# Masks of the windowed attention: from TensorE matmuls to the VectorE instruction that finds the row maximum

## The chip, the cores and the metric

The kernel runs on one core of one Trainium2 chip. The metric is the device time of one execution in microseconds (us). The version before the change takes 2654.65 us, the median of three runs (2653.8 to 2655.82). Times inside an execution are read from one profiled execution.

## The reference, cut to what matters

The program is two transformer-like layers. The change touches only the second attention, a windowed one: 4,096 rows, 16 heads of 64, windows of 128 queries, and each window attends to itself and to the window before it.

```python
sim = jnp.einsum('bhwid,bhwjd->bhwij', bq, bk)       # 128 queries x 256 keys
causal_mask = (bq_t < bq_k) | (bq_t > bq_k + ws * LOOK_BACKWARD)
sim = jnp.where(causal_mask | pad_mask, mask_value, sim)
attn = jax.nn.softmax(sim, axis=-1)
out = jnp.einsum('bhwij,bhwjd->bhwid', attn, bv)
```

So of the window before, a query sees the keys from its own position on, of its own window the keys up to its own position, and the first window of a sequence has nothing before it.

## The kernel before

The last stage, `stage_windows`, goes over 32 tiles of 128 rows (one tile is one window, all 16 heads). Heads are taken in 8 pairs. The engines run programs of their own that meet through semaphores; `window_steps` writes one list of steps that all of them follow, and the order on every engine is that of this list.

- Step `S p` (the scores of head pair p): TensorE writes 128 x 2 heads x 256 keys into one of two PSUM tiles, `pss[p % 2]` (printed as w_pss). For each half of the keys (role 0 the window before, role 1 the own window) it first multiplies the mask by the identity (L1687), which puts 0 or -1e30 into the scores, and then adds three products of the high and low parts of q and k (`PARTS`, L1689). VectorE takes the negated row maximum of both heads (L1879), and ScalarE then computes exp(score + that) with the row sum (L1791), one instruction for each head.
- The scores buffer is double, so `S p` waits until the exponentials of pair p-2 are done: `wait(pe, exp_ready, PAIRS * t + max(p - 1, 0))`.
- `N p`: VectorE takes the reciprocal of the row sums (L1885), GpSimd scales the probabilities (L1626). `T p`: TensorE turns them (L1709), VectorE (even p) or ScalarE (odd p) copies them to SBUF. `PV p`: product with v (L1730).
- `W 0..5` and `E 0..3`: projections of the next tile (L1649 with wqkv) and of the experts of this tile (L1649 with we). They stand between the S steps. ScalarE empties W (L1748), VectorE empties E (L1900, L1902). `QR`, `KR`: rotation of the next q and k on VectorE and GpSimd (L1540, L1544, L1547). `R`: their transposes (L1661), taken by ScalarE (L1757, L1761) and VectorE (L1858, L1862).
- The end of a tile: `G` and `OUT`, the output product (L1739, w_psy) on TensorE, and on VectorE the gate (L1919 to L1921) and the result (L1926, L1930). VectorE's next instruction is the maximum of `S 0` of the next tile.

The tiles are visited by a generator, `tiles`. Tiles 0 and 1 are written out, tiles 2 to 29 are a loop with two tiles in its body (semaphore values in registers), tiles 30 and 31 are written out with shorter lists of steps. The last tile has no W steps.

Of the kernel before, what the change touches and what calls it, by code (L numbers as in the profile page):

```python
# [16 lines left out]
BF16 = mybir.dt.bfloat16  # L17
# [3 lines left out]
ALU = mybir.AluOpType  # L21
# [12 lines left out]
H = 16  # L34
EPS = 1e-5
NEG = -1e30


HD = D // H
# [1424 lines left out]
def stage_windows(nc, io, keep, dram, out):  # L1464
# [6 lines left out]
    with ExitStack() as ctx:  # L1471
        st = Stage(nc, ctx, "w_")
        wqkv, we, wout = keep["wqkv"], keep["we"], keep["wout"]
        rope = st.sb("rope", [P, 2, 3, DH // 2])
        own_mask = st.sb("own_mask", [P, P], BF16)
        before_mask = st.sb("before_mask", [P, P], BF16)
        even_masks = st.sb("even_masks", [P, NT // 2, P], BF16)
        xnt = st.sb("xnt", [P, 2, KD, P])
        xr = [st.sb(f"xr{r}", [P, 2, KD, P], F32R) for r in range(2)]
        x1 = st.sb("x1", [P, 2, D])  # L1480
# [40 lines left out]

        def tiles(eng):

            for i in rounds(eng, NT // 2 - 1):
                for u in range(2):
                    yield 2 * i + u, u, i, steps
            yield NT - 2, 0, NT // 2 - 1, ending_steps
            yield NT - 1, 1, NT // 2 - 1, last_steps

        def heads(ap):  # L1530
            return ap.rearrange("p (h s x) -> p h s x", s=2, x=DH // 2)
# [45 lines left out]
        @block.gpsimd  # L1577
        def _(pool):
            ch = Chain(pool, pool_step)
            def low_rows(tile, u):  # L1580

                pool.wait_ge(x_high, tile + 1)
                pool.tensor_tensor(xr[1][:, u, :, :], xnt[:, u, :, :], xr[0][:, u, :, :].bitcast(F32), ALU.subtract  # L1583
                                   ).then_inc(x_ready, 1)

            def rotate(n, t, taken, table, landed):

                if n == 0:

                    pool.wait_ge(rope_landed[table], landed)  # L1590
                    wait(pool, work_taken["act"], taken)
                    wait(pool, t_ready, turns.filled(t))
                    wait(pool, k_rotated, t + 1)
                ins = rotary(pool, 1, n, table)
                if n < 5:
                    ch.link(ins)
                else:
                    ins.then_inc(k_rotated, 1)

            low_rows(0, 0)  # L1600

            ch.link(pool.memset(own_mask[:, :], 0.0))
            ch.link(pool.affine_select(out=own_mask[:, :], in_=own_mask[:, :], compare_op=ALU.is_ge, fill=NEG, base=0,
                                       pattern=[[-1, P]], channel_multiplier=1))
            for mask in (before_mask[:, :].unsqueeze(1), even_masks[:, :, :]):
                ch.link(pool.memset(mask, 0.0))
                ch.link(pool.affine_select(out=mask, in_=mask, compare_op=ALU.is_ge, fill=NEG, base=0,  # L1607
                                           pattern=[[0, mask.shape[1]], [1, P]], channel_multiplier=-1))
            for b in range(B):

                ch.link(pool.memset(even_masks[:, b * NT // B // 2, :], NEG))

            pool.memset(v[1][:, :], 0.0).then_inc(pool_set, 1)

            low_rows(1, 1)
            pool.wait_ge(pool_set, 1)
            for n in range(6):
                rotate(n, -1, 4, 0, 16)
            start = ch.k
            for t, u, i, order in tiles(pool):  # L1620
                ch.base, ch.k = start + t * 5, 0
                for s in order:
                    if s[0] == "N":
                        p = s[1]
                        wait(pool, inv_ready, PAIRS * t + p + 1)
                        pool.tensor_tensor(probs[:, p % 4, :, :], probs[:, p % 4, :, :],  # L1626
                                           inv[:, :, p:p + 1].to_broadcast([P, 2, 2 * P]), ALU.mult).then_inc(p_ready, 1)
                    elif s[0] == "KR":
                        rotate(s[1], t, work.emptied("act", t) + 4, 1 - u, 16 * (i + 1 + u))
                    elif s[0] == "X":  # L1630
                        low_rows(t + 2, u)

        @block.tensor
        def _(pe):
# [39 lines left out]
            for t, u, i, order in tiles(pe):  # L1674
                w = r = 0
                for s in order:
                    if s[0] == "S":
# [3 lines left out]
                            for who in ("act", "dve"):  # L1681
                                wait(pe, turn_taken[who], turns.emptied(who, t))
                        wait(pe, exp_ready, PAIRS * t + max(p - 1, 0))
                        mask = (even_masks[:, bass.ds(i, 1), :], before_mask[:, :].unsqueeze(1))[u]
                        for role, (mask, keys) in enumerate(((mask, kd[1 - u]), (own_mask[:, :].unsqueeze(1), kd[u]))):
                            scores = pss[p % 2][:, :, role * P:(role + 1) * P]
                            pe.matmul(scores, keep["identity16"][:, :], mask.to_broadcast([P, 2, P]), start=True, stop=False)  # L1687
                            for a, b in PARTS:
                                ins = pe.matmul(scores, qt[a][:, p, :], keys[b][:, p, :, :], start=False,  # L1689
                                                stop=(a, b) == PARTS[-1])  # L1690
                        ins.then_inc(s_ready, 1)
                    elif s[0] == "W":
# [50 lines left out]
        def _(act):  # L1743
            def take_work(n, t, filled, bank):

                act.wait_ge(work_ready, filled)
                wait(act, (q_rotated, k_rotated, v_moved)[n // 2], t + 1)
                act.activation(raw[:, n // 2, (n % 2) * CH:(n % 2 + 1) * CH], psw[bank][:, :], ACT.Copy,  # L1748
                               scale=DH ** -0.5 if n < 2 else 1.0).then_inc(work_taken["act"], 1)

            def high_turned(n, t, filled, bank, into):

# [24 lines left out]
            for t, u, i, order in tiles(act):  # L1777
# [4 lines left out]
                for s in order:  # L1782
                    if s[0] == "S":
                        p = s[1]
                        if p == 0:
                            wait(act, inv_ready, PAIRS * t)
                        act.wait_ge(top_ready, PAIRS * t + p + 1)

                        wait(act, t_ready, turns.filled(t) + (turns.index(order, ("T", p - 4)) + 1 if p >= 4 else 0))
                        for e in range(2):  # L1790
                            ins = act.activation(probs[:, p % 4, e, :], pss[p % 2][:, e, :], ACT.Exp, bias=top[:, e, p:p + 1],  # L1791
                                                 accum_out=rows[:, e, p:p + 1])
                        ins.then_inc(exp_ready, 1)
                        if p == 1:

                            wait(act, pv_done, PAIRS * t)
                            wait(act, work_taken["act"], work.emptied("act", t))
                            act.copy(v[u][:, :], raw[:, 2, :]).then_inc(v_moved, 1)
                    elif s[0] == "W":
                        take_work(s[1], t, work.filled(t) + w + 1, w % 2)  # L1800
                        w += 1
                    elif s[0] == "E":
                        w += 1
                    elif s[0] in ("T", "R"):
                        if s[0] == "T" and emptier(s) == "act":
                            wait(act, t_ready, turns.filled(t) + r + 1)
                            wait(act, pv_done, PAIRS * t + max(s[1] - 1, 0))
                            act.copy(pt[:, s[1] % 2, :, :], pst[r % 2][:, :, :]).then_inc(turn_taken["act"], 1)
                        elif s[0] == "R":
                            high_turned(s[1], t, turns.filled(t) + r + 1, r % 2, 1 - u)  # L1810
                        r += 1
                    elif s[0] == "X":

                        act.wait_ge(work_ready, work.filled(t + 1))
                        high_rows(t + 2, u, 16 * (i + 2))
                    elif s[0] == "PV" and s[1] % 4 == 3:
                        half = s[1] // 4
                        wait(act, pv_done, PAIRS * t + s[1] + 1)
                        if half == 0:

                            wait(act, y_ready, t)
                        act.copy(ot[:, 4 * half:4 * half + 4, :], pso[:, :, :]).then_inc(ot_ready, 1)
                    elif s[0] == "G":

                        act.wait_ge(work_taken["dve"], work.emptied("dve", t + 1))
                        wait(act, out_ready, t)
                        act.activation(sig[:, :], y[:, :], ACT.Exp, scale=-1.0).then_inc(sig_ready, 1)

        @block.vector
        def _(vec):  # L1830
# [5 lines left out]
                        ins = vec.tensor_copy(kd[u][r][:, two:two + 2, :, :], keep["zero"][:, :])  # L1836
            ins.then_inc(keys_cleared, 1)
            vec.wait_ge(keys_cleared, 1)

            def rotate(n, t, taken, table, landed):  # L1840

# [30 lines left out]
            for t, u, i, order in tiles(vec):  # L1872
                ch.base, ch.k = start + t * per_tile, 0
                w = r = 0
                for s in order:
                    if s[0] == "S":
                        p = s[1]
                        vec.wait_ge(s_ready, PAIRS * t + p + 1)
                        vec.tensor_reduce(top[:, :, p], pss[p % 2][:, :, :], X, ALU.max, negate=True).then_inc(top_ready, 1)  # L1879
                    elif s[0] == "N":  # L1880
                        p = s[1]
                        if p == 0:
# [141 lines left out]
```

## Time and profile before

| what | value |
|---|---|
| runs, median (lowest to highest) | 2654.65 us (2653.8 to 2655.82) |
| profiled execution, its own time | 2632.49 us |
| its span | 2630.8 us |
| TensorE busy | 2418.7 us, 92% |
| VectorE busy | 1848.7 us, 70% |
| ScalarE busy | 1410.8 us, 54% |
| GpSimd busy | 927.0 us, 35% |
| mean granted TensorE clock | 0.961 |

The windows stage takes the time from about 1446 us to the end of the span. Busy time of TensorE is the time in which a matmul was under way; since matmuls overlap, the starts of successive ones say what each costs.

### The profile page before, as it was taken

The page shows a single profiled execution, that of the slowest core. Times are in us where ns is not written, and L with a number is a line of the kernel's source. Part 1 is how long each engine was busy: PE and PEld are TensorE (multiplying, and loading weights), DVE is VectorE, ACT ScalarE, POOL GpSimd, SP SyncE. Part 2 cuts the span into 40 slices and gives each one's busy share as a digit, 9 for nine tenths or more (in the row PEclk, how much of TensorE's full clock was granted, in tenths as well). Part 3 has the DMA queues.
Part 4 walks back from the last instruction along what each step waited for, and adds up shares of the span by engine and source line. Part 5 has one row for each costly group of instructions (what it writes and reads, how often), then busy time and mean ns, then how long its engine had stood idle before and what let it go on. Part 6 is the DMA issues. An engine that isn't in the chain of part 4 may idle for free. (4 is left out here: it accounts for less than half of the span.)

```text
span 2630.8 us, 46834 instructions
## 1 busy us (share of the span) xinstructions
PE 2418.7 (92%) x15908; PEld 1554.5 (59%) x15908; DVE 1848.7 (70%) x3682; ACT 1410.8 (54%) x2776; POOL 927.0 (35%) x910
## 2 busy tenths in 40 slices
PE   5769999999999999699965799999999999999999
PEld 4622333333333333188855677777777777777777
DVE  7768888888888887143367577767677777777676
ACT  3514556666666666665433455554555555555544
POOL 2031010111122111043352555455554455554554
PEclk9859999999999999899976899999999999999999
DMA  3772133240413400233184000000000000000000
GB/s 124 186 173 31 17 50 40 29 61 22 63 37 61 61 24 7 85 120 121 65 267 153 13 13 14 13 13 9 11 13 13 13 13 9 11 13 13 13 10 7
DMA packets 140296, 132.47 MB, mean 50 GB/s; under 512 B 50321, under 2 KB 128151, under 8 KB 140176
## 3 DMA queue, kind: packets, MB, share of 16 engines
q1 hardware_dynamic: 110992, 101.63, 17.2%
q10 hardware_dynamic: 23680, 12.59, 1.9%
q0 software_dynamic: 5504, 16.69, 1.7%
q8 instruction: 70, 1.15, 0.2%
q14 instruction: 50, 0.41, 0.1%
HBM read 84.43 MB, written 46.14 MB: 50 GB/s over the span
## 5 line engine op out<-in xcount | busy, mean ns | idle before, releaser
L903 DVE TENSOR_REDUCE a_best<-a_ring 128x1 f32<-128x512 f32 (+3 forms) x1280 | 699.1, 603 | 138.9 <-PE a_ring L709 83.0
L815 ACT ACTIVATE a_probs<-a_pss 128x1024 f32<-128x1024 f32 (+3 forms) x640 | 556.1, 895 | 398.5 <-PE a_pss L757 388.3
L1791 ACT ACTIVATE w_probs<-w_pss,w_top 128x256 f32<-128x256 f32 x512 | 239.5, 477 | 378.1 <-DVE w_top L1879 363.7
L1626 POOL TENSOR_TENSOR w_probs<-w_probs,w_inv 128x512 f32<-128x512 f32 x256 | 301.3, 1177 | 394.3 <-DVE w_inv L1885 385.0
L668 POOL TENSOR_SCALAR_AFFINE_SELECT a_probs<-a_probs 128x256 f32<-128x256 f32 x256 | 102.9, 408 | 773.3 <-ACT a_probs L815 771.5
L1649 PE MATMUL w_psw<-wqkv,w_xr 128*128 128x512 f32 x1152 | 300.3, 397 | 11.6 <-POOL w_xr L1583 11.6
L1689 PE MATMUL w_pss<-w_kd,w_qt 128*128 128x256 f32 x1536 | 277.6, 309 | 0.0
L1879 DVE TENSOR_REDUCE w_top<-w_pss 128x2 f32<-128x512 f32 x256 | 176.8, 691 | 140.7 <-PE w_pss L1689 139.7
L709 PE MATMUL a_ring<-g_kb,g_qa 96*128 96x512 bf16 (+3 forms) x640 | 227.7, 369 | 47.6 <-PEq L221 30.0
L709 PE MATMUL a_ring<-a_kb,a_qa 96*128 96x512 bf16 (+3 forms) x640 | 218.4, 350 | 16.0 <-DVE a_best L903 12.2
L1649 PEld LDWEIGHTS w_psw<-wqkv,w_xr 128*128 128x128 f32 x1152 | 204.6, 189 | 47.3 <-POOL w_xr L1583 12.1
L1689 PEld LDWEIGHTS w_pss<-w_kd,w_qt 128*128 128x128 f32 x1536 | 221.3, 195 | 4.1
L757 PE MATMUL a_pss<-g_qa,g_kb 99*128 99x512 bf16 (+3 forms) x640 | 217.2, 352 | 3.3 <-ACT a_probs L815 1.7
L757 PE MATMUL a_pss<-a_qa,a_kb 99*128 99x512 bf16 (+3 forms) x640 | 206.7, 350 | 1.0 <-ACT a_probs L815 0.6
L1649 PE MATMUL w_psw<-we,w_xr 128*128 128x512 f32 x768 | 204.2, 401 | 0.0
L1730 PE MATMUL w_pso<-w_pt,w_v 128*64 128x128 f32 x2048 | 168.3, 285 | 0.1
L1709 PE MATMUL w_pst<-identity,w_probs 128*128 128x128 f32 x1024 | 155.7, 275 | 0.0
L776 PE MATMUL a_acc<-a_probs,a_vg 128*32 128x512 f32 (+3 forms) x1280 | 150.9, 543 | 0.8 <-POOL a_probs L668 0.7
L776 PE MATMUL a_acc<-a_probs,g_vg 128*32 128x512 f32 (+3 forms) x1280 | 150.9, 543 | 0.0
L757 PEld LDWEIGHTS a_pss<-g_qa,g_kb 99*128 99x128 bf16 x640 | 60.8, 98 | 148.8 <-ACT a_probs L815 98.6
L1649 PEld LDWEIGHTS w_psw<-we,w_xr 128*128 128x128 f32 x768 | 134.9, 188 | 22.9 <-issue 0.2
L757 PEld LDWEIGHTS a_pss<-a_qa,a_kb 99*128 99x128 bf16 x640 | 57.2, 97 | 151.0 <-ACT a_probs L815 105.8
(232 smaller groups left out, 4170.2 us busy)
## 6 DMA issues: line engine op xcount, KB each, us to landing
e_w<-in_w SPq DMA_DIRECT2D x16, 1024.0 KB, 7.8
qk_parts<-p_parts SPq DMA_DIRECT2D x32, 384.0 KB, 3.9
g_kb<-qk_parts SPq DMA_DIRECT2D x24, 256.0 KB, 8.9
g_qa<-qk_parts SPq DMA_DIRECT2D x96, 64.0 KB, 13.2
a_kb<-qk_parts SPq DMA_DIRECT2D x24, 256.0 KB, 8.6
a_qa<-qk_parts SPq DMA_DIRECT2D x96, 64.0 KB, 13.6
p_xin<-in_x SPq DMA_DIRECT2D x8, 512.0 KB, 5.3
v_rows<-p_vout SPq DMA_DIRECT2D x8, 512.0 KB, 5.2
```

Source lines behind the costliest of these rows:

```text
L709: ins = pe.matmul(bank[:, 0:keys], qa[u][0:QR, i // TC, h, (i % TC) * P:(i % TC + 1) * P], kb[u][0:QR, h, k * CH:k * CH + keys], start=Tru ...
L757: ins = pe.matmul(pss[idx % 2][:, e, lo:CH], kb[u][0:MR, h, j * P:(j + 1) * P], qa[u][0:MR, c, h, lo:CH], start=True, stop=True)
L776: ins = pe.matmul(acc[32 * h:32 * h + 32, lo:CH], vg[u][:, j, h, :], probs[:, 2 * (pv % 2) + h // 2, h % 2, lo:CH], start=(j == 0), stop=( ...
L815: act.activation(probs[:, idx % 4, :, lo:CH], pss[idx % 2][:, :, lo:CH], ACT.Exp).then_inc(exp_done, 1)
L903: vec.tensor_reduce(best[:, i // TC, h * TC + i % TC, k:k + 1], bank[:, 0:keys], X, ALU.max).then_inc(ring_taken, 1)
L1626: pool.tensor_tensor(probs[:, p % 4, :, :], probs[:, p % 4, :, :], inv[:, :, p:p + 1].to_broadcast([P, 2, 2 * P]), ALU.mult).then_inc(p_re ...
L1649: ins = pe.matmul(psw[bank][:, :], xr[a][:, src, k, :], moving(b, k), start=(m == 0), stop=(m == len(pairs) - 1))
L1689: ins = pe.matmul(scores, qt[a][:, p, :], keys[b][:, p, :, :], start=False, stop=(a, b) == PARTS[-1])
L1709: ins = pe.transpose(pst[r % 2][:, 2 * e + role, :], probs[:, p % 4, e, role * P:(role + 1) * P], keep["identity"][:, :])
L1730: ins = pe.matmul(pso[e * DH:(e + 1) * DH, p % 4, :], v[(u + 1 + role) % 2][:, h * DH:(h + 1) * DH], pt[:, p % 2, 2 * e + role, :], start= ...
L1791: ins = act.activation(probs[:, p % 4, e, :], pss[p % 2][:, e, :], ACT.Exp, bias=top[:, e, p:p + 1], accum_out=rows[:, e, p:p + 1])
L1879: vec.tensor_reduce(top[:, :, p], pss[p % 2][:, :, :], X, ALU.max, negate=True).then_inc(top_ready, 1)
```

## The change

The mask leaves TensorE. A mask of float32 with 0 and +1e30 lies in SBUF, for both kinds of tile. The projections of q are scaled by -1/8 instead of 1/8, so the scores come negated. VectorE adds the mask to a head's negated scores in place in PSUM and takes the minimum of the sums in the same instruction, which is the negated maximum that ScalarE needs as its bias; ScalarE's exponential then takes scale -1. This instruction handles one head (256 scores), the old one handled two (512). The generator `tiles` yields all 32 tiles, so no loop is left in this stage. VectorE waits once for the masks to be set.

```diff
-        own_mask = st.sb("own_mask", [P, P], BF16)
-        before_mask = st.sb("before_mask", [P, P], BF16)
-        even_masks = st.sb("even_masks", [P, NT // 2, P], BF16)
+        masks = st.sb("masks", [P, 2, 2, P])
...
-            for i in rounds(eng, NT // 2 - 1):
-                for u in range(2):
-                    yield 2 * i + u, u, i, steps
-            yield NT - 2, 0, NT // 2 - 1, ending_steps
-            yield NT - 1, 1, NT // 2 - 1, last_steps
+            for t in range(NT):
+                yield t, t % 2, t // 2, steps if t < NT - 2 else (ending_steps, last_steps)[t % 2]
+
+        def mask_of(t):
+
+            first = t % (NT // B) == 0
+            return masks[:, 0 if first else 1, :, :].rearrange("p r k -> p (r k)")
...
-                            pe.matmul(scores, keep["identity16"][:, :], mask.to_broadcast([P, 2, P]), start=True, stop=False)
                             for a, b in PARTS:
-                                ins = pe.matmul(scores, qt[a][:, p, :], keys[b][:, p, :, :], start=False,
+                                ins = pe.matmul(scores, qt[a][:, p, :], keys[b][:, p, :, :], start=(a, b) == PARTS[0],
                                                 stop=(a, b) == PARTS[-1])
...
-                               scale=DH ** -0.5 if n < 2 else 1.0).then_inc(work_taken["act"], 1)
+                               scale=-DH ** -0.5 if n < 2 else 1.0).then_inc(work_taken["act"], 1)
...
-                                                 accum_out=rows[:, e, p:p + 1])
+                                                 scale=-1.0, accum_out=rows[:, e, p:p + 1])
...
             vec.wait_ge(keys_cleared, 1)
+            vec.wait_ge(pool_set, 1)
...
-                        vec.tensor_reduce(top[:, :, p], pss[p % 2][:, :, :], X, ALU.max, negate=True).then_inc(top_ready, 1)
+                        for e in range(2):
+                            scores = pss[p % 2][:, e, :]
+                            ins = vec.tensor_tensor_reduce(out=scores, in0=scores, in1=mask_of(t), scale=1.0, scalar=HIGHEST,
+                                                           op0=ALU.add, op1=ALU.min, accum_out=top[:, e, p:p + 1])
+                        ins.then_inc(top_ready, 1)
```

What it moves in the program order. On TensorE, the steps `S 0` and `W 0` of tile 0, before:

```order
L1687 MATMUL w_pss<-w_even_masks,identity 128x2x128
L1689 MATMUL w_pss<-w_kd_0,w_qt 128x2x128
L1689 MATMUL w_pss<-w_kd_1,w_qt 128x2x128
L1689 MATMUL w_pss<-w_kd_0,w_qt 128x2x128
L1687 MATMUL w_pss<-w_own_mask,identity 128x2x128
L1689 MATMUL w_pss<-w_kd_0,w_qt 128x2x128
L1689 MATMUL w_pss<-w_kd_1,w_qt 128x2x128
L1689 MATMUL w_pss<-w_kd_0,w_qt 128x2x128
L1649 MATMUL w_psw<-wqkv,w_xr 128x512 x6
```

and the same place of the changed kernel (its lines are two to four lower):

```order
L1685 MATMUL w_pss<-w_kd_0,w_qt 128x2x128
L1685 MATMUL w_pss<-w_kd_1,w_qt 128x2x128
L1685 MATMUL w_pss<-w_kd_0,w_qt 128x2x128 x2
L1685 MATMUL w_pss<-w_kd_1,w_qt 128x2x128
L1685 MATMUL w_pss<-w_kd_0,w_qt 128x2x128
L1647 MATMUL w_psw<-wqkv,w_xr 128x512 x6
```

Two of eight matmuls of each S step are gone; nothing else moves on this engine. On VectorE, from the maximum of `S 3` to that of `S 4` of tile 0, before:

```order
L1879 TENSOR_REDUCE w_top<-w_pss 128x2
L1885 RECIPROCAL w_inv<-w_rows 128x2
L1540 TENSOR_TENSOR w_crossed<-w_raw,w_rope 128x16x32
L1913 COPY w_pt<-w_pst 128x512
L1879 TENSOR_REDUCE w_top<-w_pss 128x2
```

and of the changed kernel, where ISA is how the new instruction is printed, and the second ISA row of each pair is the one that writes its minimum to w_top:

```order
L1878 ISA w_pss,w_top<-w_pss,w_masks 128x256
L1878 ISA w_top 128x1
L1878 ISA w_pss,w_top<-w_pss,w_masks 128x256
L1878 ISA w_top 128x1
L1886 RECIPROCAL w_inv<-w_rows 128x2
L1542 TENSOR_TENSOR w_crossed<-w_raw,w_rope 128x16x32
L1914 COPY w_pt<-w_pst 128x512
L1878 ISA w_pss,w_top<-w_pss,w_masks 128x256
```

One instruction of 512 scores has become four: two of 256 scores and two that write one number. On GpSimd, at the start of the stage, before:

```order
L1583 TENSOR_TENSOR w_xr<-w_xnt,w_xr 128x256
L1602 MEMSET w_own_mask 128x128
L1603 AFFINE_SELECT w_own_mask<-w_own_mask 128x128
L1606 MEMSET w_before_mask 128x128
L1607 AFFINE_SELECT w_before_mask<-w_before_mask 128x128
L1606 MEMSET w_even_masks 128x2048
L1607 AFFINE_SELECT w_even_masks<-w_even_masks 128x2048
L1611 MEMSET w_even_masks 128x128 x2
L1613 MEMSET w_v 128x1024
```

and of the changed kernel:

```order
L1585 TENSOR_TENSOR w_xr<-w_xnt,w_xr 128x256
L1604 MEMSET w_masks 128x512
L1605 AFFINE_SELECT w_masks<-w_masks 128x2x128
L1607 AFFINE_SELECT w_masks<-w_masks 128x128
L1609 MEMSET w_masks 128x128
L1611 MEMSET w_v 128x1024
```

The masks that were made for each even tile, 2048 columns, are gone, and four shorter instructions stand where eight did.

## Rows read from the trace of the kernel before

**Rows 1.** The page: span, and busy time of each engine.

```profile
span 2630.8 us, 46834 instructions
PE 2418.7 (92%) x15908; PEld 1554.5 (59%) x15908; DVE 1848.7 (70%) x3682; ACT 1410.8 (54%) x2776; POOL 927.0 (35%) x910
```

**Rows 2.** Stretches (tile 1, a looped one): PE, PEld, DVE, ACT, POOL busy; PEclk; DMA; GB/s.

```profile
1512.90:1549.00 36.10, 36.10 (x253) 28.71 (x252) 25.54 (x46) 19.34 (x53) 18.96 (x15) 1.00 0.05 13
2051.40:2087.55 36.15, 36.15 (x256) 28.74 (x252) 25.61 (x46) 19.35 (x54) 19.02 (x15) 1.00 0.04 12
```

**Rows 3.** Timeline of TensorE in the looped tile: start, us, engine, instruction.

```profile
2055.16 0.27 PE L1687 MATMUL w_pss<-w_even_masks,identity 128*128 x1
...
2056.10 1.56 PE L1649 MATMUL w_psw<-wqkv,w_xr 128*128 128x512 f32 x6
...
2059.85 0.28 PE L1687 MATMUL w_pss<-w_even_masks,identity 128*128 x1
...
2084.85 0.66 PE L1709 MATMUL w_pst<-identity,w_probs 128*128 128x128 f32 x4
```

**Rows 4.** Timeline of TensorE in the experts stage: 256-column matmuls in one row.

```profile
1231.22 9.01 PE L1046 MATMUL e_psy<-e_w_r,e_hidden 128*128 128x256 f32 x73 [0.89 <-DVE e_hidden L1104]
```

**Rows 5.** Timeline of VectorE in the looped tile.

```profile
2057.65 0.69 DVE L1879 TENSOR_REDUCE w_top<-w_pss 128x2 f32<-128x512 f32 x1
...
2066.13 0.69 DVE L1879 TENSOR_REDUCE w_top<-w_pss 128x2 f32<-128x512 f32 x1 [0.25 <-PE w_pss L1689]
2066.74 0.16 DVE L1885 RECIPROCAL w_inv<-w_rows 128x2 f32<-128x2 f32 x1
2066.81 0.67 DVE L1540 TENSOR_TENSOR w_crossed<-w_raw,w_rope 128x512 f32<-128x512 f32 x1
```

**Rows 6.** Timelines of TensorE, VectorE and ScalarE in tile 1, which is written out.

```profile
1512.86 0.27 PE L1687 MATMUL w_pss<-w_before_mask,identity 128*128 128x256 bf16 x1
...
1515.19 0.68 DVE L1879 TENSOR_REDUCE w_top<-w_pss 128x2 f32<-128x512 f32 x1
...
1515.96 0.47 ACT L1791 ACTIVATE w_probs<-w_pss,w_top 128x256 f32<-128x256 f32 x1 [4.67 <-issue]
...
1516.33 0.19 ACT L1791 ACTIVATION_READ_ACCUMULATOR w_probs<-w_pss,w_top 128x1 f32 x1
1516.43 0.47 ACT L1791 ACTIVATE w_probs<-w_pss,w_top 128x256 f32<-128x256 f32 x1
1516.78 0.20 ACT L1791 ACTIVATION_READ_ACCUMULATOR w_probs<-w_pss,w_top 128x1 f32 x1
```

**Rows 7.** The last tile: ScalarE frees a scores buffer, TensorE goes on.

```profile
2601.25 0.20 ACT L1791 ACTIVATION_READ_ACCUMULATOR w_probs<-w_pss,w_top 128x1 f32 x1
...
2601.50 0.28 PE L1687 MATMUL w_pss<-w_before_mask,identity 128*128 128x256 bf16 x1 [2.11 <-ACT w_probs L1791]
```

**Rows 8.** Groups of VectorE by shape, whole span: busy, mean ns | idle before.

```profile
L903 DVE TENSOR_REDUCE a_best<-a_ring 128x1 f32<-128x256 f32 x128 | 53.2, 416 | 13.5 <-PE a_ring L712 13.3
...
L1926 DVE TENSOR_TENSOR w_res<-w_psy,w_sig 128x256 f32<-128x256 f32 x32 | 13.6, 424 | 2.9 <-PE w_psy L1739 0.5
...
L155 DVE TENSOR_TENSOR_SCAN j_r_scanned<-running,j_r_total 128x256 f32<-128x256 f32 x1 | 0.7, 691 | 0.0
```

**Rows 9.** Timelines at the start of the stage: GpSimd, ScalarE, VectorE.

```profile
1457.52 1.42 DVE L1540 TENSOR_TENSOR w_crossed<-w_raw,w_rope 128x512 f32<-128x512 f32 x2 [5.76 <-ACT w_raw L1748]
...
1459.17 1.10 POOL L1583 TENSOR_TENSOR w_xr<-w_xnt,w_xr 128x256 fp32r<-128x256 f32 x1
1459.51 0.60 ACT L1748 ACTIVATE w_raw<-w_psw 128x512 f32<-128x512 f32 x1 [0.76 <-PE w_psw L1649]
1460.28 1.69 POOL L1540 TENSOR_TENSOR w_crossed<-w_raw,w_rope 128x512 f32<-128x512 f32 x1
```

**Rows 10.** Timeline of GpSimd in the looped tile: the last scaling of probabilities.

```profile
2081.57 1.04 POOL L1626 TENSOR_TENSOR w_probs<-w_probs,w_inv 128x512 f32<-128x512 f32 x1
```

**Rows 11.** The page: the DMA queue that brings instructions.

```profile
q8 instruction: 70, 1.15, 0.2%
```

More of the change, by code:

```diff
@@ L36 @@
 NEG = -1e30
+FAR = 1e30
+HIGHEST = 3.0e38
 HD = D // H
@@ L1600, in _ @@
             low_rows(0, 0)
[L1602 to L1611, printed above, removed]
+            ch.link(pool.memset(masks[:, :, :, :], 0.0))
+            ch.link(pool.affine_select(out=masks[:, :, 1, :], in_=masks[:, :, 1, :], compare_op=ALU.is_ge, fill=FAR, base=0,
+                                       pattern=[[0, 2], [-1, P]], channel_multiplier=1))
+            ch.link(pool.affine_select(out=masks[:, 1, 0, :], in_=masks[:, 1, 0, :], compare_op=ALU.is_ge, fill=FAR, base=0,
+                                       pattern=[[1, P]], channel_multiplier=-1))
+            ch.link(pool.memset(masks[:, 0, 0, :], FAR))
             pool.memset(v[1][:, :], 0.0).then_inc(pool_set, 1)
@@ L1683, in _ @@
                         wait(pe, exp_ready, PAIRS * t + max(p - 1, 0))
-                        mask = (even_masks[:, bass.ds(i, 1), :], before_mask[:, :].unsqueeze(1))[u]
-                        for role, (mask, keys) in enumerate(((mask, kd[1 - u]), (own_mask[:, :].unsqueeze(1), kd[u]))):
+                        for role, keys in enumerate((kd[1 - u], kd[u])):
                             scores = pss[p % 2][:, :, role * P:(role + 1) * P]
-                            pe.matmul(scores, keep["identity16"][:, :], mask.to_broadcast([P, 2, P]), start=True, stop=False)
                             for a, b in PARTS:
-                                ins = pe.matmul(scores, qt[a][:, p, :], keys[b][:, p, :, :], start=False,
+                                ins = pe.matmul(scores, qt[a][:, p, :], keys[b][:, p, :, :], start=(a, b) == PARTS[0],
                                                 stop=(a, b) == PARTS[-1])
```

## The prediction

> **What bounds the kernel now.** I read the page first: TensorE is busy 92% of the span and VectorE 70% [rows 1]. A share over many stages does not say what the windows stage waits for, so I took stretches of one tile next [rows 2]. In tile 1 and in a tile of the loop TensorE is busy for the whole stretch, 36.10 of 36.10 and 36.15 of 36.15 us, at granted clock 1.00 (the level of 2.4 GHz); VectorE has 25.6 us of work, ScalarE 19.4, GpSimd 19.0. The reader is to see two things. A tile costs what its matmuls cost, and a tile that is written out costs the same as one in the loop, so the unrolling alone gives TensorE nothing. TensorE's matmuls are what the change cuts, VectorE's work is what it grows, so the question is how much of the cut VectorE's later answer takes back.
>
> **The matmuls removed.** Each S step loses two of its eight matmuls. The step takes from 2055.16 to the first W matmul at 2056.10, 0.94 us [rows 3]; an equal share is 0.1175 us each, so two cost 0.235. The other reading is what remains: 73 matmuls of 256 columns in one row take 9.01 us in the experts stage, of which the last is 0.28 by itself, so (9.01 - 0.28) / 72 = 0.121 us from start to start [rows 4] (0.28 is the length that a 256-column matmul shows [rows 7]). Six of them are 0.73, which leaves 0.21. I take 0.225 for each S step; 8 steps in 32 tiles are 256 steps, so 57.6 us, with 54 and 60 as the ends. These rows also show that six weight loads in a row keep up at this pace.
>
> **The new VectorE instruction.** The old one lasts 0.69 us and the next may start 0.61 after its start (2066.13 to 2066.74); the small one behind it holds the engine 0.07 (2066.74 to 2066.81) [rows 5]. No row shows the new one. Nearest are a maximum over 256 elements of PSUM, 0.416 us, and an operation of one PSUM and one SBUF operand of 256, 0.424 us [rows 8]. With the same overlap of 0.08 each holds the engine for 0.34. The number behind it is an instruction of its own; ScalarE's counterpart lasts 0.20 and the next instruction starts 0.10 after it (1516.33 to 1516.43) [rows 6]. So a pair holds VectorE for 2 x (0.34 + 0.10) = 0.88 and its last number is there after L = 0.34 + 0.10 + 0.34 + 0.20 = 0.98 us; with 0.07 for the small one, a pair is at 0.82 and L at about 0.91. I take L = 0.95 against 0.69 before. The low end is no cost for the extra instruction, L = 0.34 + 0.42 = 0.76. The high end is the scan of 256 elements, also two operands and a running value, at 0.691 [rows 8]: L = 0.61 + 0.10 + 0.61 + 0.20 = 1.52. I stay near the low rows because a minimum needs only a comparison per element as the maximum does.
>
> Where nothing holds the next instruction it starts before the one ahead has ended, 0.61 after the start of one of 0.69 [rows 5]. The Trainium skill says otherwise, and so speaks against splitting (VectorE: DVE Perf Modes, section "The DRAIN you can't avoid"): after every operation the pipe is emptied before the next one starts. This trace disagrees; by the rule the sum below would be 45 us instead of 51.
>
> **Where it lands on the path.** VectorE's answer matters where TensorE has least to do between a scores step and the one that reuses its buffer: `S 2` of each tile, with only `S 1`, `W 0` and `W 1` between, and at a time when VectorE is still busy with the gate and the result of the tile before. In the loop the maximum of `S 0` starts at 2057.65, 2.49 us after `S 0` began, and `S 2` begins at 4.69 [rows 3, 5]. In tile 1, without register arithmetic, it starts 1515.19 - 1512.86 = 2.33 after `S 0`, and the second read by ScalarE ends at 1516.78 + 0.20 = 1516.98, that is 4.12 after [rows 6]. This is where the unrolling helps: it gives 0.16 us back, worth nothing before since `S 2` began later anyhow. From the end of that read to TensorE's start are 0.05 us (2601.25 + 0.20 to 2601.50) [rows 7]. After the change `S 2` could begin at 4.69 - 2 x 0.225 = 4.24, and its buffer is free at 4.12 + 0.05 + (L - 0.68). The new stall is L - 0.75, for L = 0.95 it is 0.20 us in each tile with a tile before it. The gate before it starts from copies that hang on TensorE's last steps, so it does not come earlier than now.
>
> Elsewhere the added work is covered. From `S 3` on a T and a PV step stand between, some 1 us more. VectorE's load in a tile grows by 8 x (0.85 - 0.61) = 1.9 to about 27.5 us of a tile that shrinks to about 34.5. Between `S 4` and `S 7`, where it also rotates, it falls a few tenths behind and catches up at the end of the tile. GpSimd ends its last scaling at 2082.61, and TensorE turns that pair at 2084.85, 2.2 us later [rows 3, 10]; the four S steps from 4 to 7 shrink by 0.9 in all, which leaves 1.3. If that cover were gone, each tenth would cost 3 us over the stage.
>
> **The start of the stage, and the new wait.** The GpSimd instructions for the masks get fewer and shorter. But the first rotation of k at 1460.28 also waits for ScalarE's copy of the fourth projection, which ends at 1459.51 + 0.60 = 1460.11 [rows 9], so at most 0.2 us comes of it. VectorE's wait for the masks stands ahead of its first rotation, which starts at 1457.52 and waits for ScalarE; the masks and the v clearing behind them are set before, so nothing is queued by it. The scales on ScalarE change no shape. These count as nothing.
>
> **The sum.** 57.6 - 30 x 0.20 (tiles 1 to 30) = 51.6. The last tile has no W steps, so its `S 2` waits for the exponentials already (2.11 us idle [rows 7]) and gets the full 0.27 of L, with the two steps before it hidden: -0.7 from the gain. That makes 51 us. The profiled execution's 2632.5 becomes 2581.5. The runs' median lies 22.2 us above the profiled time, and I carry this over: 2654.65 - 51 = 2603.6, say 2604 us. For L from 0.86 to 1.05 and matmuls at 0.21 to 0.235 it is 2599 to 2609.
>
> **The rivals.**
> - *No stall.* L is at its low end of 0.76: the full 57 to 60 us, 2595 to 2598. For it: the rows of 256 elements. Against it: the extra instruction is there in the program order.
> - *Each instruction waits for the one before it to end.* L = 0.42 + 0.16 + 0.42 + 0.16 = 1.16 (0.16 is the small operation's length [rows 5]), stall 0.41, gain 56.9 - 12.3 = 44.6: 2610. A row against it is named above, but a read of what the instruction before has accumulated may well be held when an independent one is not. It is the way of the emptied pipe in the Trainium skill's page named above.
> - *Two cycles for each element,* as the scan shows. L = 1.52, stall 0.77 at `S 2`. A pair then holds VectorE for 1.42, a tile has 25.6 + 8 x (1.42 - 0.61) = 32.1 us of work in some 35, the copies of turned probabilities come late, and I put another 0.1 to 0.3 on that. Per tile 1.80 - 0.97 = 0.83, in all about 26 us: 2628.
> - *Slower: the written-out code is fetched too late.* 28 tiles that were 14 rounds of a loop are now fetched once each. A packet of the instruction queue takes 0.002 x 16 x 2630.8 / 70 = 1.2 us and brings 16 KB [rows 11]. It decides from 1.6 us lost in a tile. Were each tile to wait for two such packets (my choice), 2.4 us, the kernel would be slower by 28 x 0.8 = 22 us: 2677. Against it: tile 1 is written out too, needs its code fetched just so, and runs at 36.10 [rows 2].
> - *Nothing measurable:* VectorE's late work meets another wait of 1.6 us or more per tile that I don't see. About 2654.
>
> **How the numbers follow.** Chances: forecast 0.50, no stall 0.10, each waits 0.14, two cycles 0.18, slower by fetching 0.05, nothing 0.03. A change of 0.2% (5.3 us) is about what a measurement of this kernel can tell from none. The range runs from 2595, the low end of the case without a stall, up to 2630, which takes in most of the two-cycle case. Faster: the first four, 0.92; same 0.03; slower 0.05.
>
> **What would show it.** In the changed trace: no matmuls on masks, S steps of 0.70 to 0.73 us, a steady tile of 34.5 us (36.15 - 1.80 + 0.20), the new instruction at 0.42 us twice and a small one behind each, TensorE idle 0.2 us before `S 2` and released by ScalarE's exponential, and nowhere else. The first thing to doubt is L: a length of 0.7 speaks for two cycles, and a start of the small one only at the end of the large one for the waiting case. A tile that varies in length from one to the next, with idle put down to issue, would speak for the fetch.

## The result, and the profile after

The changed kernel takes 2612.18 us (median of 4 runs, 2610.82 to 2614.31) where the kernel before takes 2654.4 us in the runs beside it: a ratio of 0.9837, 95% interval 0.9822 to 0.9852. It is 42 us faster; 51 were forecast, and the time lies in the forecast range of 2595 to 2630, though above the 2599 to 2609 that the forecast gave for its own case.

The profiled execution of the changed kernel spans 2610.7 us against 2630.8 [rows 1], which looks like 20 us and not 42. The stages ahead of the windows, which the change doesn't touch, differ between the two profiles. (The record does not name their chips. The kernel before takes 2634 to 2635 us on each of the three chips of the experiments, close to its profiled 2632.5 and not to its timed 2654.4, so the profiles probably come from two chips.) Stretches split at the first matmul of the windows stage show it; columns as in [rows 2]. The kernel before:

```profile
0.00:1452.40 1452.40, 1255.52 (x7844) 629.45 (x7845) 1029.65 (x2242) 791.32 (x1082) 313.87 (x423) 0.94 0.35 82
1452.40:2630.80 1178.40, 1163.18 (x8064) 925.07 (x8064) 819.00 (x1440) 619.52 (x1694) 613.11 (x488) 0.99 0.04 12
```

and the changed one:

```profile
0.00:1474.10 1474.10, 1268.70 (x7844) 630.72 (x7844) 1029.14 (x2242) 791.11 (x1082) 314.07 (x423) 0.93 0.34 80
1474.10:2610.70 1136.60, 1121.07 (x7552) 906.12 (x7552) 860.48 (x2208) 612.25 (x1694) 607.03 (x484) 0.99 0.05 13
```

The first parts differ by 21.7 us with the same 7,844 matmuls. The windows stage goes from 1178.40 to 1136.60, that is 41.8 us less, which is the timed difference. So only this stage is compared from here on. TensorE lost 512 matmuls and 42.1 us of busy time, VectorE gained 41.5.

The page of the changed kernel, its line of busy times and the groups of the changed instructions:

```profile
PE 2389.8 (92%) x15396; PEld 1536.8 (59%) x15396; DVE 1889.6 (72%) x4450; ACT 1403.4 (54%) x2776; POOL 921.1 (35%) x906
...
L1787 ACT ACTIVATE w_probs<-w_pss,w_top 128x256 f32<-128x256 f32 x512 | 241.0, 482 | 363.0 <-DVE w_top L1878 211.9
...
L1878 DVE CUSTOM_DVE_ANT_0 w_pss<-w_pss,w_masks 128x256 f32<-128x256 f32 x512 | 206.2, 449 | 87.5 <-PE w_pss L1685 87.4
```

and from its groups by shape the small instruction behind each:

```profile
L1878 DVE DVE_READ_ACCUMULATOR2_ANT w_top<- 128x1 f32 x512 | 72.0, 141 | 0.0
```

The new instruction takes 449 ns for 256 scores, like the cheap rows of [rows 8] and not like the scan. A steady tile is 34.84 us, where [rows 2] had 36.15; TensorE is still busy for all of it, at granted clock 1.00:

```profile
2017.26:2052.10 34.84, 34.84 (x238) 28.14 (x236) 26.91 (x70) 19.13 (x53) 18.99 (x15) 1.00 0.05 14
```

Here is the start of that tile on VectorE, ScalarE and TensorE's weight loads (PEld), the place of [rows 5, 6]:

```profile
2022.93 0.42 DVE L1931 TENSOR_TENSOR w_res<-w_res,w_x 128x256 f32<-128x256 f32 x1
...
2023.28 0.42 DVE L1878 CUSTOM_DVE_ANT_0 w_pss<-w_pss,w_masks 128x256 f32<-128x256 f32 x1
...
2023.62 0.14 DVE L1878 DVE_READ_ACCUMULATOR2_ANT w_top<- 128x1 f32 x1
2023.62 0.47 DVE L1878 CUSTOM_DVE_ANT_0 w_pss<-w_pss,w_masks 128x256 f32<-128x256 f32 x1
...
2024.00 0.14 DVE L1878 DVE_READ_ACCUMULATOR2_ANT w_top<- 128x1 f32 x1
2024.00 0.47 DVE L1878 CUSTOM_DVE_ANT_0 w_pss<-w_pss,w_masks 128x256 f32<-128x256 f32 x1
...
2024.23 0.48 ACT L1787 ACTIVATE w_probs<-w_pss,w_top 128x256 f32<-128x256 f32 x1 [4.85 <-issue]
...
2025.05 0.20 ACT L1787 ACTIVATION_READ_ACCUMULATOR w_probs<-w_pss,w_top 128x1 f32 x1
...
2025.30 0.30 PEld L1685 LDWEIGHTS w_pss<-w_kd,w_qt 128*128 128x128 f32 x2 [0.43 <-ACT w_probs L1787]
```

The second large instruction starts 0.34 us after the first, and the next pair of heads 0.38 after that; the two results are there 2024.00 + 0.14 - 2023.28 = 0.86 us after the start (L, forecast 0.95). TensorE's load for `S 2` then starts 0.05 after ScalarE's second read. And the scores steps on TensorE, each with the W or E step behind it:

```profile
2023.04 0.88 PE L1685 MATMUL w_pss<-w_kd,w_qt 128*128 128x256 f32 x6
2023.75 1.55 PE L1647 MATMUL w_psw<-wqkv,w_xr 128*128 128x512 f32 x6
2025.30 0.98 PE L1685 MATMUL w_pss<-w_kd,w_qt 128*128 128x256 f32 x6
2026.12 1.55 PE L1647 MATMUL w_psw<-wqkv,w_xr 128*128 128x512 f32 x6
2027.51 0.87 PE L1685 MATMUL w_pss<-w_kd,w_qt 128*128 128x256 f32 x6
2028.21 1.59 PE L1647 MATMUL w_psw<-wqkv,w_xr 128*128 128x512 f32 x6
...
2033.31 0.98 PE L1685 MATMUL w_pss<-w_kd,w_qt 128*128 128x256 f32 x6
2034.13 1.56 PE L1647 MATMUL w_psw<-wqkv,w_xr 128*128 128x512 f32 x6
```

The reader is to take differences of starts. `S 1` and `S 3` last 0.71 and 0.70 us, as forecast. `S 2` starts 1.55 after the W step ahead of it where 1.39 is the rule, so 0.16 of waiting, and lasts 0.82. `S 5`, which waits for nothing, also lasts 0.82, and so do `S 6` and `S 7`. This 0.11 was not in the forecast. The experiments are about it and about the wait. Of 30 tiles 29 last 34.81 to 34.85 us; the second lasts 35.05, and the extra 0.22 is more idle time at its `S 2`, ended by ScalarE's exponential.

### The profile page after: what moved, and what is told of

Read it like the earlier page. It is cut to its first block and busy times, and to the rows that moved or that the text cites. A ratio compares the mean times of both kernels' runs of the same rounds, so it can differ in the third digit from the quotient of the medians.

```text
span 2610.7 us, 43417 instructions
## 1 busy us (share of the span) xinstructions
PE 2389.8 (92%) x15396; PEld 1536.8 (59%) x15396; DVE 1889.6 (72%) x4450; ACT 1403.4 (54%) x2776; POOL 921.1 (35%) x906
## 3 DMA queue, kind: packets, MB, share of 16 engines
q8 instruction: 119, 1.95, 0.3%
## 5 line engine op out<-in xcount | busy, mean ns | idle before, releaser
L1878 DVE CUSTOM_DVE_ANT_0 w_pss<-w_pss,w_masks 128x256 f32<-128x256 f32 x512 | 206.2, 449 | 87.5 <-PE w_pss L1685 87.4
L1685 PE MATMUL w_pss<-w_kd,w_qt 128*128 128x256 f32 x1536 | 248.1, 298 | 6.4 <-DVE w_kd L1859 3.3
L1685 PEld LDWEIGHTS w_pss<-w_kd,w_qt 128*128 128x128 f32 x1536 | 207.7, 191 | 43.3 <-ACT w_probs L1787 21.1
```

Of the source, the lines that this page charges most:

```text
L1878: ins = vec.tensor_tensor_reduce(out=scores, in0=scores, in1=mask_of(t), scale=1.0, scalar=HIGHEST, op0=ALU.add, op1=ALU.min, accum_out=to ...
```

## The experiments

**The kernel before, again.** No edit. Expected:

> The kernel before, once more with a profile. Theory: the profiled execution of before was 22 us shorter than its timed runs because of the first attention, not of the windows stage. Then this profile has a steady tile of 36.15 us again and 1178 us from the first windows matmul to the end of the span, while the stages ahead of it may take either 1452 us or some 20 us more. Rival: the windows stage itself differs between executions, which would show as another tile length and would make the comparison of tiles between before and after unsafe.

It took 2634.01 us, beside a median of 2634.08 for before on that chip; the tile is 36.15 us throughout. The windows stage takes 1179.10 us, within 1 us of the other profile:

```profile
1453.30:2632.40 1179.10, 1164.14 (x8064) 925.77 (x8064) 818.88 (x1440) 619.49 (x1694) 612.65 (x488) 0.99 0.04 12
```

So tiles can be compared between profiles, and whole executions only beside runs of before on the same chip. Why the changed kernel's first profile is 20 us longer ahead of the windows stays open. Most of it lies from 600 to 1000 us: TensorE has 2434 matmuls there at granted clock 0.97, and 2551 at 1.00 in the profile of before. What lowers the clock no run shows.

**Only the tiles written out**, masks as before:

```diff
-            for i in rounds(eng, NT // 2 - 1):
-                for u in range(2):
-                    yield 2 * i + u, u, i, steps
...
+            for t in range(NT):
+                yield t, t % 2, t // 2, steps if t < NT - 2 else (ending_steps, last_steps)[t % 2]
```

> Only the loop is written out, masks stay on TensorE. Theory: nothing, tile 36.15 us as in the loop, 2654 us within 3. VectorE's maximum of the first pair starts about 0.1 us earlier after the tile's first scores and gets no credit. Rival (the loop's register work or its branch costs time that the profile hides): 5 us or more faster. Rival (code fetched late): slower, idle put down to issue in single tiles.

Ratio 0.9999 (0.9984 to 1.0014), tile 36.15 us. VectorE's first maximum of a tile starts 1.39 us after `W 0` begins, where the loop has 1.52 (means over 23 tiles), and this gets no credit, as expected. Writing the loop out is worth nothing by itself, and its code is not fetched too late.

**No masks at all**, one maximum over both heads, written out. Its output is that of an attention over all keys:

```diff
-                            pe.matmul(scores, keep["identity16"][:, :], mask.to_broadcast([P, 2, P]), start=True, stop=False)
                             for a, b in PARTS:
-                                ins = pe.matmul(scores, qt[a][:, p, :], keys[b][:, p, :, :], start=False,
+                                ins = pe.matmul(scores, qt[a][:, p, :], keys[b][:, p, :, :], start=(a, b) == PARTS[0],
```

> Masks left out altogether (so the attention is over all 256 keys), VectorE keeps its one maximum over 512 scores, tiles written out: the cut on TensorE alone. Theory: no stall at S 2 (its buffer is free 0.1 us before it is wanted), but the exposed loads in S 5 to S 7 stay: tile 34.6 us, about 0.25 us less than in the changed kernel, 2604 us. Rival (VectorE's instruction costs nothing and all of the 0.28 us per tile above the forecast is weight loads): 34.83 us as in the changed kernel, 2612 us. Rival (the forecast's price of a matmul was wrong and no load is exposed): 34.3 us.

Ratio 0.9824 (0.9802 to 0.9846), 2585.81 us where before takes 2634.08, and a tile of 34.63 us: 0.20 less than in the changed kernel. This is what VectorE's new instruction costs, measured. But the cut on TensorE alone is 36.15 - 34.63 = 1.52, not 1.80. Its `S 2` shows part of why; weight loads, then matmuls:

```profile
2036.12 0.20 ACT L1787 ACTIVATION_READ_ACCUMULATOR w_probs<-w_pss,w_top 128x1 f32 x1
...
2036.37 0.78 PEld L1685 LDWEIGHTS w_pss<-w_kd,w_qt 128*128 128x128 f32 x6 [0.26 <-ACT w_probs L1787]
2036.38 0.98 PE L1685 MATMUL w_pss<-w_kd,w_qt 128*128 128x256 f32 x6
...
2037.20 1.55 PE L1646 MATMUL w_psw<-wqkv,w_xr 128*128 128x512 f32 x6
```

Its matmuls start in time (1.38 after the W step) and yet the step lasts 0.82. The buffer came free at 2036.12 + 0.20 = 2036.32, too late for the load to run ahead of the matmuls. In `S 3` of the changed kernel it does run ahead: the load starts at 2027.28, the matmuls at 2027.51.

```profile
2027.28 0.90 PEld L1685 LDWEIGHTS w_pss<-w_kd,w_qt 128*128 128x128 f32 x6
```

So a wait that costs no idle time can still expose a load.

**The mask multiplied last** in the kernel before, for the half that heads the step. Same matmuls, but a float32 load of q heads the step instead of the bf16 load of the identity:

```diff
-                            pe.matmul(scores, keep["identity16"][:, :], mask.to_broadcast([P, 2, P]), start=True, stop=False)
+                            if role == 1:
+                                pe.matmul(scores, keep["identity16"][:, :], mask.to_broadcast([P, 2, P]), start=True, stop=False)
                             for a, b in PARTS:
...
+                            if role == 0:
+                                pe.matmul(scores, keep["identity16"][:, :], mask.to_broadcast([P, 2, P]), start=False, stop=True)
```

> The kernel before, with the mask of the window before multiplied after its three score products instead of ahead of them. The same 8 matmuls in a step, but a float32 weight load now heads the step instead of the bf16 load of the identity. Theory (the head's weight load can't start behind a PV step and is exposed): 0.10 us more in S 5, S 6 and S 7, a tile of about 36.45 us, 9 to 10 us slower than before, 2664 us. Rival (what was not gained in these steps has to do with VectorE, PSUM or the pace of six loads in a row): no change, 36.15 us, 2654 us.

Ratio 1.0026 (1.0014 to 1.0037), tile 36.32. Slower with the same work, as the theory has it, but by 0.17 and not 0.30 a tile. The steps say why. Behind a PV step, from 2073.97 to 2075.02:

```profile
2073.97 0.63 PE L1690 MATMUL w_pss<-w_kd,w_qt 128*128 128x256 f32 x3
2074.44 0.28 PE L1693 MATMUL w_pss<-w_even_masks,identity 128*128 x1
2074.56 0.27 PE L1688 MATMUL w_pss<-w_own_mask,identity 128*128 128x256 bf16 x1
2074.59 0.60 PE L1690 MATMUL w_pss<-w_kd,w_qt 128*128 128x256 f32 x3
2075.02 1.54 PE L1649 MATMUL w_psw<-wqkv,w_xr 128*128 128x512 f32 x6
```

it lasts 1.05 against 0.95, the 0.10 that was expected, three times in a tile. The scores steps behind W and most projection steps each got 0.01 to 0.03 shorter, some 0.13 in a tile, which had not been thought of; why is not shown.

**PV with full-width loads** in the changed kernel: weights of 128 columns instead of 64, so both heads' products are mixed and the output is another:

```diff
-                                ins = pe.matmul(pso[e * DH:(e + 1) * DH, p % 4, :], v[(u + 1 + role) % 2][:, h * DH:(h + 1) * DH],
+                                ins = pe.matmul(pso[:, p % 4, :], v[(u + 1 + role) % 2][:, p * P:(p + 1) * P],
...
```

> The changed kernel with PV matmuls that load all 128 columns of a pair's v instead of 64 and write all 128 partitions (both heads' products mixed, so the attention's output is another). Theory (a scores step's first load is exposed because the PV step ahead of it loads only half of the array's columns): S 5 to S 7 take 0.71 us, the time behind a W step, instead of 0.82. Rival (it is exposed behind any float32 PV step, whatever its width, or for its short matmuls): still 0.82. The tile itself gets longer by the wider PV matmuls, which says nothing.

One run, 2617.62 us; the tile is 35.54 because the wider PV steps cost more. The step lasts 0.79, neither the expected 0.71 nor 0.82; its length alone doesn't decide, because its first matmul can now be recorded earlier. The two steps together do: a wide PV step lasts 0.81 ahead of a scores step and 0.89 ahead of an R step, and 0.81 + 0.79 is 0.89 + 0.71, so nothing of the load is exposed. The narrow PV step lasts 0.59 ahead of either, and 0.82 follows it. The weight loads show where it comes from. The changed kernel, T, PV and `S 5`:

```profile
2031.96 0.59 PEld L1705 LDWEIGHTS w_pst<-identity,w_probs 128*128 128x128 f32 x4
2032.72 0.42 PEld L1726 LDWEIGHTS w_pso<-w_pt,w_v 128*64 128x64 f32 x8 [0.17 <-issue]
2033.31 0.77 PEld L1685 LDWEIGHTS w_pss<-w_kd,w_qt 128*128 128x128 f32 x6 [0.17 <-issue]
```

with full-width PV:

```profile
2060.10 0.59 PEld L1705 LDWEIGHTS w_pst<-identity,w_probs 128*128 128x128 f32 x4
2060.66 0.97 PEld L1726 LDWEIGHTS w_pso<-w_pt,w_v 128*128 128x128 f32 x8
2061.55 0.78 PEld L1685 LDWEIGHTS w_pss<-w_kd,w_qt 128*128 128x128 f32 x6
```

and the same place of the kernel before:

```profile
2067.85 0.42 PEld L1730 LDWEIGHTS w_pso<-w_pt,w_v 128*64 128x64 f32 x8 [0.17 <-issue]
2068.44 0.10 PEld L1687 LDWEIGHTS w_pss<-w_even_masks,identity 128*128 128x128 bf16 x1 [0.17 <-issue]
2068.45 0.43 PEld L1689 LDWEIGHTS w_pss<-w_kd,w_qt 128*128 128x128 f32 x3
```

Behind the narrow loads there is a gap of 0.17 us; behind the wide ones the next load starts at once. The gap stands on both sides of PV: the first narrow load behind the 128-column loads of T is 0.17 late as well, and that gap too is gone with full-width PV (a T step ahead of PV then lasts 0.44 instead of 0.53). Inside a PV step, from one narrow load to the next, there is none. So a load does not run ahead where the width of the weights changes, in either direction. That it is the width and not the float32 passes, this pair shows, and the gap behind the full-width matmuls of T speaks against the short matmuls of PV as its cause; what in the array makes it so, no run shows.

**PV ahead of T** in the changed kernel, so that a scores step stands behind a transpose:

```diff
-        if p >= 3:
-            steps.append(("T", p - 3))
         if p >= 4:
             steps.append(("PV", p - 4))
+        if p >= 3:
+            steps.append(("T", p - 3))
```

> The changed kernel with the order of two steps swapped: PV p-4 now stands ahead of T p-3, so each scores step from S 5 on stands behind a transpose instead of behind a PV step. Theory (only a load behind a PV step is exposed): S 5 to S 7 lose their 0.10 us, the transpose behind PV may take over some 0.06 of it (a T step behind PV lasts 0.66 against 0.60): tile 34.65 to 34.8 us, 1 to 6 us faster than the changed kernel's 2612. Rival (any change of matrix shape exposes the same): 34.83 us, 2612.

Ratio 0.9812 (0.9784 to 0.984), tile 34.62: 0.21 less, a little more than expected. From one scores step to the next are 3.27 us, where it was 3.33. So the swap gives back 0.06 of the 0.11 in each; T now stands behind PV and pays most of the rest. The last tile, which has no W steps, pays: from the last output product but one to the last are 30.33 us instead of 29.3.

**The result of a tile later** on VectorE, behind the minimum of the next tile's first pair, in the changed kernel (L1927 and L1931 move into `finish`):

```diff
                         ins.then_inc(top_ready, 1)
+                        if held:
+                            finish(*held.pop())
...
+                        held.append((t, u, i))
+                        if t == NT - 1:
+                            finish(*held.pop())
```

> The changed kernel, but VectorE computes the result of a tile (two instructions, L1927 and L1931) after the minimum of the next tile's first pair instead of ahead of it. So that minimum starts 0.8 us earlier. Theory (the stall at S 2, 0.15 us idle and 0.10 us of exposed load, comes from VectorE's late answer): both go, tile 34.6 us, 7 to 8 us faster than the changed kernel, 2604 us. Rival (S 2 waits for something else, such as ScalarE's copies or the bank of W): 34.83 us, 2612.

Ratio 0.9814 (0.979 to 0.9837), tile 34.53: 0.30 less. Of this 0.27 is at `S 2`, where the wait of 0.16 and the exposed load of 0.11 are gone; 0.02 more comes from the W step behind `S 3` (1.40 instead of 1.42):

```profile
2037.28 1.55 PE L1647 MATMUL w_psw<-wqkv,w_xr 128*128 128x512 f32 x6
2038.67 0.88 PE L1685 MATMUL w_pss<-w_kd,w_qt 128*128 128x256 f32 x6
2039.38 1.55 PE L1647 MATMUL w_psw<-wqkv,w_xr 128*128 128x512 f32 x6
```

The W step ahead of `S 2` takes 1.39 again, and `S 2` lasts 0.71. The timed ratios of this kernel and of the one before it overlap with the changed kernel's own, 0.9837 and 0.984; it is the tile, the same within 0.04 us in nearly all of 30, that tells them apart.

**Both edits together:**

> The two edits before together. If the two losses are separate they add up: tile 34.4 to 34.6 us, 2597 to 2604 us. If one covers the other, no better than the better one alone.

Ratio 0.9773 (0.9747 to 0.9798), 2575.65 us where before takes 2635.38; tile 34.33. The two add up: 0.21 + 0.30 against 0.50 measured, just below the expected 34.4 to 34.6. This is the best kernel of the study, 0.7% ahead of the changed one by their ratios to before.

**The changed kernel again**, on the chip of the full-width run and of the run below:

> The changed kernel once more, on the chip of these runs and beside its runs of before. Every theory expects a tile of 34.83 us; the ratio is 0.984, about 2593 us where before takes 2635. If the difference between chips were in the windows stage too, the tile would differ.

Ratio 0.984 (0.9823 to 0.9856), 2591.49 us, tile 34.83 as in the first profile.

**A later answer of VectorE:**

```diff
+                        if p == 0 and t > 0:
+                            for k in range(2):
+                                vec.memset(spare[:, k, :], 0.0)
                         vec.wait_ge(s_ready, PAIRS * t + p + 1)
```

> The changed kernel with two clears of two numbers on VectorE ahead of the minimum of each tile's first pair, about 0.14 to 0.16 us, as much as the loop's registers delayed it. Theory (VectorE's answer to S 0 sets S 2, one for one; so writing out the tiles is worth about 0.15 us a tile in the changed kernel, though nothing in the kernel before): tile 34.97 to 34.99 us. Rival (the delay is absorbed): 34.83 us.

One run, 2583.82 us, tile 34.75 us. It tells nothing: the clears ran beside the addition ahead of them, and the minimum started only 0.02 us later than without them, so there was no delay to test. The tile came out 0.08 us shorter, which no theory says; each of `S 5` to `S 7` and the projection step behind it were 0.02 shorter together. What writing out the tiles is worth in the changed kernel was therefore not measured; a looped version of it was not tried.

## Why the forecast came out right, and its gain 9 us too high

Gain in a steady tile, us, from differences of starts (means over 23 tiles):

| term | forecast | measured | from |
|---|---|---|---|
| two matmuls fewer in eight S steps, loads hidden | 1.80 | 1.95 | 8 x 0.244, the mean of `S 0`, `S 1`, `S 3`, `S 4` |
| float32 load exposed behind PV, S 5 to S 7 | 0 | -0.33 | each gains 0.13 and not 0.244 |
| S 2: waiting and its load | -0.20 | -0.30 | 34.83 - 34.53 |
| sum | 1.60 | 1.32 | 36.15 - 34.83 |

The 1.95 is an estimate: no kernel has all eight steps with hidden loads. The two edits together reach 36.15 - 34.33 = 1.82: with T behind PV, each of `S 5` to `S 7` and the T step ahead of it still gain only 0.20.

- *What bounds the kernel:* right. TensorE is busy for all of a tile before and after, and the timed gain is that of its steps.
- *The cut:* where the load is hidden a step gains 0.23 to 0.26, somewhat more than the 0.225 of the forecast: `S 1` and `S 3` went from 0.956 to 0.71. The forecast had read the old length at `S 0`, 0.94, the shorter case, and the new one as 0.73 from the experts stage. **The step that failed is the sentence that rows 4 "show that six weight loads in a row keep up at this pace".** They do keep up; but the row says nothing of the first load of a step. Until now that was the short bf16 load of the identity (0.10 us against 0.19), and the removed mask matmul had hidden the first float32 load behind itself. Mask last, full-width PV and PV ahead of T each show this. It is 0.33 us a tile, 10.6 us in all, of which PV ahead of T gives back 0.20 a tile.
- *VectorE's instruction:* L was 0.86 for 0.95, inside 0.76 to 1.05. The number behind the large instruction is read 0.34 to 0.38 us after its start and costs VectorE almost nothing. The cases of waiting instructions and of two cycles are out.
- *Where it lands:* right in place. The stall was to be L - 0.75, 0.11 with the measured L; 0.16 of idle time is there. The path from VectorE to the free buffer is the forecast's within 0.01 us; what differs is that `S 2` could begin 0.04 earlier, since the two scores steps ahead of it shrank by more than 0.225. The load that a late wait exposes adds another 0.11, which the forecast did not have. The no-masks kernel, with the old maximum, has part of this exposed load too; against it the changed kernel loses 0.20, the very figure of the forecast, but for an L of 0.86 and not 0.95: that they agree is luck.
- *The cover elsewhere:* VectorE's work is 26.9 us of 34.84 (27.5 of 34.5 forecast). No other step of TensorE is held up by more than the 0.02 us of the W step behind `S 3`.
- *The whole stage:* to the forecast's sum of 51 us the measured terms add 32 x 0.15 = 4.7 for the larger cut, take off 32 x 0.33 = 10.6 for the load behind PV and 30 x 0.10 = 3.0 for the larger loss at `S 2`, and give 42.1. The windows stage measured 41.8: 39.5 in the 30 tiles from the first output product to the 31st, 1.4 ahead of them and 0.9 behind. So the forecast is off by 9 us and not by 14 because one error ran against the others.
- *The rivals:* fetching the code late is refuted by the written-out kernel (0.9999). By its time alone, 2612 us, the run would look like the rival in which each instruction waits for the one before it (2610); the rows exclude that, since its L was 1.16 and 0.86 is there. The section of the Trainium skill that the forecast set beside this rival (VectorE: DVE Perf Modes, "The DRAIN you can't avoid") also says that a next instruction that is not held starts earlier; the forecast left this out, and the starts 0.34 and 0.38 us after instructions of 0.42 and 0.47 agree with it.
- *The range:* it reached up to 2630 to take in the two-cycle case, which did not come, and so covered an error of another kind. The narrower 2599 to 2609 missed the time; by its own terms (0.21 and L = 1.05) its upper end should have been 2610.

## What to carry to other kernels

Where one engine is busy all the time, a removed instruction gives back its start-to-start time, but look also at what it hid: here a small instruction at the head of a step was what let the first large load run ahead. When work is moved to an engine that is idle on average, look for the cost where its answer is waited for: here VectorE's 41 us of added work cost 0.20 us a tile, and moving two unrelated instructions behind that answer bought 0.30. And check that two profiles agree in the stages that the change doesn't touch before their spans are compared.

## What was unexpected of the hardware

- Where the width of the weights changed, from 128 to 64 columns or back, the first weight load started 0.17 us late; with PV at 128 columns the gaps were gone. A scores step behind the 64-column PV cost 0.11 us more for it, and T ahead of PV 0.09.
- On VectorE an instruction that accumulates and the read of its accumulator overlap: the next large instruction is recorded at the same moment as that read (2023.62), and a pair held the engine for 0.72 us (2023.28 to 2024.00), little more than one maximum over 512 (0.61 [rows 5]).
- Ahead of the windows stage, where both kernels run the same code, one profile took about 20 us more than the others.
